# State-space layers: step sizes by way of PSUM, spread of C at the begin of its phase, u in the bank of z, another order of the work

## The reference, cut to what matters

```python
xz = x @ in_w
u, z = jnp.split(xz, 2, axis=-1)
uc = cb + sum((up[:, k:k + L, :] * cw[:, k] for k in range(D_CONV)))
u = jax.nn.silu(uc)
proj = u @ xpw                      # dt (8), Bm (16), Cm (16)
delta = jax.nn.softplus(dt @ dtw + dtb)
def step(h, inp):
    dA = jnp.exp(d_t[..., None] * A)
    h = dA * h + (d_t * u_t)[..., None] * b_t[:, None, :]
    y = jnp.einsum('bdn,bn->bd', h, c_t)
y = (ys + u * Dp) * jax.nn.silu(z)
x = _layer_norm(y @ ow + x, ln_w[i], ln_b[i])
```

## Time and profile before

| | us |
|---|---|
| median of three runs | 626.53 |
| the three runs | 626.53, 624.88, 626.65 |
| the profiled execution | 624.93 |
| its span in the trace | 623.1 |

### The profile page before, as it was taken

How to read it: one execution, slowest core, us unless ns; L and a number is a source line. 1 busy time by engine, 2 the same in 40 slices (tenths; PEclk the granted TensorE clock), 3 DMA queues, 4 the chain that set the end, 5 groups by cost and what they waited for, 6 DMA issues and landing times.

```text
span 623.1 us, 21724 instructions
## 1 busy us (share of the span) xinstructions
PE 525.9 (84%) x8989; PEld 416.4 (67%) x8989; DVE 442.8 (71%) x1737; ACT 322.1 (52%) x952; POOL 147.9 (24%) x197
## 2 busy tenths in 40 slices
PE   6979968779995999999999999997588888888668
PEld 4646644468883888888888888885466666566355
DVE  2888749865445777777777777772489889898851
ACT  2778748236554344444444444343567766678411
POOL 4255625137001000000000000000624656335500
PEclk9979979699995555555555555555599999999775
DMA  8910000010003000000000000000000000000000
GB/s 317 420 50 1 3 5 1 2 49 1 1 0 103 4 5 4 4 4 4 5 4 5 4 5 4 4 5 1 1 1 2 1 3 2 2 1 2 1 1 8
DMA packets 6306, 16.13 MB, mean 26 GB/s; under 512 B 2680, under 2 KB 3488, under 8 KB 5696
## 3 DMA queue, kind: packets, MB, share of 16 engines
q1 hardware_dynamic: 5792, 14.48, 6.3%
q10 hardware_dynamic: 416, 0.26, 0.1%
HBM read 14.61 MB, written 0.13 MB: 24 GB/s over the span
## 4 chain that ended last, share of the span: by engine, by line
PE 42%; DVE 33%; ACT 15%; issue 8%; POOL 1%; DMA 1%; DVEq 0%; ACTq 0%; POOLq 0%
PE bank L1713 7%; PE bank L1807 6%; ACT esp L699 3%; PE bank L1643 3%; PE bank L1656 3%; DVE ssum L1233 2%; ACT a L686 2%; PE bank L1511 2%; DVE w L1288 2%; ACT e L701 2%; DVE qblk L1288 2%; PE bank L1919 2%; PE bank L1905 2%; DVE rz L1268 2%; DVE opre L1209 2%
## 5 line engine op out<-in xcount | busy, mean ns | idle before, releaser
L1713 PE MATMUL bank<-esp,qblk 128*128 128x1 f16 (+1 forms) x2048 | 66.6, 166 | 12.0 <-ACT esp L699 12.0
L1713 PEld LDWEIGHTS bank<-esp,qblk 128*128 128x128 f16 x2048 | 61.2, 104 | 17.3 <-ACT esp L699 17.3
L1713 PE MATMUL bank<-hsp,kT 128*128 128x2 f16 x2048 | 63.5, 166 | 2.0 <-DVE hsp L1261 1.9
L1713 PEld LDWEIGHTS bank<-hsp,kT 128*128 128x128 f16 x2048 | 59.5, 104 | 2.1 <-issue 2.1
L686 ACT ACTIVATE a<-opre 128x4 f32<-128x4 f32 x64 | 13.1, 205 | 80.8 <-DVE opre L1212 80.8
L488 POOL MEMSET ctxT<- 128x128 f32 x1 | 0.3, 313 | 229.7 <-DVE xres L1275 229.7
L693 ACT ACTIVATE gact<-bank,lgate 128x16 f32<-128x16 f32 x64 | 17.5, 274 | 45.6 <-PE bank L1713 45.6
L1288 DVE TENSOR_TENSOR_SCAN qblk<-ctxT,bank 128x512 f32<-128x512 f32 x32 | 36.8, 1202 | 3.9 <-PE bank L1905 3.6
L1288 DVE TENSOR_TENSOR_SCAN w<-kT,bank 128x512 f32<-128x512 f32 x32 | 36.7, 1201 | 1.9 <-PE bank L1905 1.6
L509 POOL TENSOR_TENSOR kT<-T,aneg 128x496 f32<-128x496 f32 x32 | 32.2, 1040 | 20.1 <-DVE T L1367 20.1
L1713 PEld LDWEIGHTS bank<-asp,lsp 128*128 128x128 f16 x768 | 25.4, 105 | 17.1 <-DVE asp L1223 16.8
(11 more groups left out here) (333 smaller groups left out, 1379.4 us busy)
## 6 DMA issues: line engine op xcount, KB each, us to landing
w<-in_w_dram SPq DMA_DIRECT2D x2, 2048.0 KB
ctxT<-in_ctxT_dram SPq DMA_DIRECT2D x8, 256.0 KB, 6.3
wqkv<-in_qkvT_dram SPq DMA_DIRECT2D x1, 1536.0 KB, 12.1
w<-in_mw_dram SPq DMA_DIRECT2D x1, 1024.0 KB, 4.8
lw<-in_lw_dram SPq DMA_DIRECT2D x1, 960.0 KB, 24.2
rows<-in_rows_dram SPq DMA_DIRECT2D x1, 772.0 KB, 8.9
wqkv<-in_fw_dram SPq DMA_DIRECT2D x1, 532.0 KB, 3.7
T<-in_mask_dram SPq DMA_DIRECT2D x1, 512.0 KB, 6.2
```

The source lines that it names most:

```text
L1713: return pe.matmul(out, lhsT, rhs, start=start, stop=stop, skip_group_check=True)
```

## The change

Step sizes: `steps_of_time` writes `m_dps`, the free half of PSUM bank 5; `times_u` reads it there, and a new VectorE instruction, `copied_steps`, copies it to `delta` in SBUF for GpSimd, which waits for that copy. `du` is signalled first, the copy second. The turned x and u move from bank 5 to bank 6, so the bias of the time steps can be put into bank 5 at the begin of a phase. `turn_c` writes to bank 6, behind the turning of du, and both it and `spread_c` now run at the begin of the phase that uses them. `spread_c` stands between `centred` and `normalised`. On TensorE, `turned` newly waits for the spread, `project_z` for `padded_u`, `time_bias` for the copied steps; `conv_bias` stands behind `turned`, `project_z` behind the second `scan_input`, `skip_y` ahead of states 5 to 7, `turn_du` behind `project_out`. On VectorE, `gate` comes ahead of the steps, and `ratio` behind the copy of state 3. On ScalarE, exp 1 stands behind `turned_x`, exp 2 behind `padded_u`, exp 5 behind the sigmoid of u, and the copy of state 6 ahead of `squares`.

```diff
 TURNED_ACT, TURNED_DVE = B * (XG - 1), B
+BY_ACT, BY_DVE = (0, 2, 4, 6), (1, 3, 5, 7)
 m_in = w1[:, 0:ML * 2 * MI]
...
 m_inv = m_a1 = bank[6][:, TOK:2 * TOK]
+m_dps = bank[5][:, TOK:2 * TOK]
...
                            pat(own4, [[0, NG], [1, BT], [0, CK]]), ALU.mult).then_inc(sem["m_dg"], 1)
-        pool.wait_ge(sem["m_delta"], 2 * c + 1)
+        pool.wait_ge(sem["m_delta"], 2 * c + 2)
         for i in range(NT):
...
     def turned_x(c):
         act.wait_ge(sem["m_xt"], c + 1)
-        act.activation(m_xT[c % 2], bank[5][:, 0:P], ACT.Copy).then_inc(sem["m_xp"], 1)
+        act.activation(m_xT[c % 2], bank[6][:, 0:P], ACT.Copy).then_inc(sem["m_xp"], 1)
     def padded_u(c):
         act.wait_ge(sem["m_uz"], 2 * c + 1)
-        act.activation(upad[:, c % 2, :, :, MK - 1:], bank[5][:, P:P + TOK].rearrange("p (c b t) -> p c b t", c=MC, b=BT),
+        act.activation(upad[:, c % 2, :, :, MK - 1:], bank[6][:, TOK:2 * TOK].rearrange("p (c b t) -> p c b t", c=MC, b=BT),
                        ACT.Copy).then_inc(sem["m_up"], 1)
     def sigmoid(to, of):
...
         c = q + 1 if q + 1 < 2 * ML else None
-        decays(q, 0, 2)
+        decays(q, 0, 1)
         if q:
...
             turned_x(c)
-        decays(q, 2, 3)
+        decays(q, 1, 2)
         if c:
             padded_u(c)
-        decays(q, 3, 4)
+        decays(q, 2, 4)
         turned_state(q, 0)
-        decays(q, 4, 6)
+        decays(q, 4, 5)
         if c:
             sigmoid_u(c)
-        decays(q, 6, 7)
+        decays(q, 5, 7)
         if c:
...
         turned_state(q, 4)
+        turned_state(q, 6)
         if c:
             squares(c)
-        turned_state(q, 6)
         turned_y(q)
...
         dve.tensor_tensor(diagcc[c % 2].rearrange("p (n t) -> p n t", t=S),
-                          pat(bank[4][:, 0:1], [[1, MN], [0, S]], TOK + 2 * MN),
+                          pat(bank[6][:, 0:1], [[1, MN], [0, S]]),
                           pat(m32, [[0, MN], [1, S]]), ALU.mult).then_inc(sem["m_prod"], 1)
     def ratio(c):
...
     def steps_of_time(c):
-        dve.scalar_tensor_tensor(out=delta, in0=bank[5][:, 0:TOK], scalar=0.0, in1=m_a2,
-                                 op0=ALU.max, op1=ALU.add).then_inc(sem["m_delta"], 1)
+        step.mark(dve.scalar_tensor_tensor(out=m_dps, in0=bank[5][:, 0:TOK], scalar=0.0, in1=m_a2,
+                                           op0=ALU.max, op1=ALU.add))
     def times_u(c):
-        dve.wait_ge(sem["m_delta"], 2 * c + 1)
-        dve.tensor_tensor(du, delta, m_gate_u[c % 2], ALU.mult).then_inc(sem["m_delta"], 1)
+        step.sync()
+        dve.tensor_tensor(du, m_dps, m_gate_u[c % 2], ALU.mult).then_inc(sem["m_delta"], 1)
+    def copied_steps(c):
+        step.sync()
+        dve.tensor_copy(delta, m_dps).then_inc(sem["m_delta"], 1)
...
     gated_z(0)
-    spread_c(0)
     ratio(0)
...
     times_u(0)
+    copied_steps(0)
     for q in range(2 * ML):
...
             centred(q - 1)
+        spread_c(q)
+        if q:
             normalised(q - 1)
...
         scan(q, 7)
+        turned_state(q, 3)
         if c:
             ratio(c)
-            spread_c(c)
-        turned_state(q, 3)
         turned_state(q, 5)
...
             second_factor(c)
-            steps_of_time(c)
         gate(q)
         if c:
+            steps_of_time(c)
             times_u(c)
+            copied_steps(c)
         residual(q)
...
             pe.wait_ge(sem["ln_xn"], LN_LAST + c)
-        pe.transpose(bank[5][:, 0:P], xn[:, c % 2, :], ident).then_inc(sem["m_xt"], 1)
+        if c:
+            pe.wait_ge(sem["m_prod"], 3 * c)
+            pe.wait_ge(sem["m_duT"], c)
+        pe.transpose(bank[6][:, 0:P], xn[:, c % 2, :], ident).then_inc(sem["m_xt"], 1)
     def project_u(c):
...
             at = (l * 2 * MC + n) * P
-            ins = mm(bank[5][:, (n + 1) * P:(n + 2) * P], m_in[:, at:at + P], m_xT[s], start=(n == 0), stop=True)
+            ins = mm(bank[6][:, (n + 2) * P:(n + 3) * P], m_in[:, at:at + P], m_xT[s], start=(n == 0), stop=True)
         ins.then_inc(sem["m_uz"], 1)
     def project_z(c):
         l, s = divmod(c, 2)
-        if c:
-            pe.wait_ge(sem["m_duT"], c)
+        pe.wait_ge(sem["m_up"], c + 1)
         at = (l * 2 + 1) * MI
...
     def time_bias(c):
-        pe.wait_ge(sem["m_up"], c + 1)
+        if c:
+            pe.wait_ge(sem["m_delta"], 2 * c)
         biases(bank[5], ML * MC + c // 2 * MC)
     def project_bc(c):
...
     def turn_c(c):
         pe.wait_ge(sem["m_dg"], 2 * c + 2)
+        pe.wait_ge(sem["m_duT"], c + 1)
         for n in range(NG):
-            ins = mm(bank[4][n * S:(n + 1) * S, TOK + 2 * MN:TOK + 3 * MN], m32, m_bcm[:, n * MN:(n + 1) * MN],
+            ins = mm(bank[6][n * S:(n + 1) * S, 0:MN], m32, m_bcm[:, n * MN:(n + 1) * MN],
                      start=True, stop=True)
...
     def turn_du(c):
-        pe.wait_ge(sem["m_delta"], 2 * c + 2)
+        pe.wait_ge(sem["m_delta"], 2 * c + 1)
         for ch in range(MC):
...
         ins.then_inc(sem["m_dt"], 1)
+    def copied_state(q, i):
+        if i in BY_ACT:
+            pe.wait_ge(sem["turned_act"], TURNED_ACT + q * len(BY_ACT) + BY_ACT.index(i) + 1)
+        else:
+            pe.wait_ge(sem["turned_dve"], TURNED_DVE + q * len(BY_DVE) + BY_DVE.index(i) + 1)
     def scan_input(q, ch):
...
             if q:
-                pe.wait_ge(sem["turned_act"], TURNED_ACT + q * BT)
-                pe.wait_ge(sem["turned_dve"], TURNED_DVE + q * BT)
+                copied_state(q - 1, BY_ACT[-1])
+                copied_state(q - 1, BY_DVE[-1])
         for b in range(BT):
...
         elif i < BT:
-            own, base = ("turned_act", TURNED_ACT) if i % 2 else ("turned_dve", TURNED_DVE)
-            pe.wait_ge(sem[own], base + q * BT + (i + 1) // 2)
+            copied_state(q, i - 1)
         for k in range(CK):
...
     def skip_y(q):
         l, s = divmod(q, 2)
-        pe.wait_ge(sem["m_prod"], 3 * min(q + 2, 2 * ML))
+        if q + 1 < 2 * ML:
+            pe.wait_ge(sem["m_bcs"], q + 2)
         if q:
...
     def sum_y(q, ch):
-        pe.wait_ge(sem["turned_act"], TURNED_ACT + q * BT + 2 * (ch + 1))
-        pe.wait_ge(sem["turned_dve"], TURNED_DVE + q * BT + 2 * (ch + 1))
+        pe.wait_ge(sem["m_prod"], 3 * q + 3)
+        for by in (BY_ACT, BY_DVE):
+            copied_state(q, max(i for i in by if i // BT == ch))
         for k in range(CK):
...
     conv_bias(0)
+    time_bias(0)
     turned(0)
...
     project_z(0)
-    time_bias(0)
     project_time(0)
     project_bc(0)
-    turn_c(0)
     turn_du(0)
...
         if c:
-            conv_bias(c)
+            time_bias(c)
+        turn_c(q)
         scan_input(q, 0)
...
             turned(c)
+            conv_bias(c)
             project_u(c)
...
         turn_state(q, 1)
+        scan_input(q, 1)
         if c:
             project_z(c)
-        scan_input(q, 1)
-        if c:
-            time_bias(c)
         turn_state(q, 2)
...
             project_bc(c)
-        for i in range(3, 7):
+        for i in range(3, 5):
             turn_state(q, i)
-        if c:
-            turn_c(c)
-        turn_state(q, 7)
         skip_y(q)
+        for i in range(5, 8):
+            turn_state(q, i)
         sum_y(q, 0)
...
         turn_y(q)
+        project_out(q)
         if c:
             turn_du(c)
-        project_out(q)
...
     pe.wait_ge(sem["ln_xT"], transposed(LN_LAST + 1 + 2 * ML))

```

## The result

The changed kernel took 620.47 us (median of 20 runs) against 625.52 for the kernel before (20 runs); the ratio of the two is 0.9924, with a 95% interval of 0.9908 to 0.9939. That is 4.75 us by the ratio and 5.05 by the medians; the forecast was 4.05. The profiled execution took 621.16 (span 619.4). Two of the changed kernel's 20 runs took 626.6 and 626.9 while the others lie between 618.5 and 622.5; one run of the kernel before took 989.56, which a median does not feel.

The account below looks back on a forecast made before the run. VectorE, busy 17.27 of 19.10 us in a steady phase, was taken as nearly full. Six phases −3.0, first phase −1.15, last +0.1 gave −4.05: 622.5 us against a median of 626.53, range 618.5 to 628.

Parts of the forecast that it names:

- Spread of C moved: VectorE, each phase: 0.60 us saved in the last stretch, normalised 0.10 later because the spread now stands before it.
- Steps, du, copy: VectorE behind the gate: du 0.42 instead of 1.07, copy about 0.40, all beside the output projection; residual 0.25 earlier.
- du behind the output projection: TensorE turns du as the projection drains (0.44); the scan input ends at G+4.2, tying with the first scan.
- GpSimd later: GpSimd's multiplies start 1.55 later; scans stall 0.17 and 0.04 behind exps 1 and 2, at no cost.
- Fifth scan, +0.12: VectorE, steady phase: the fifth scan starts at G+10.26 against 10.14, behind the second scan input.
- The slower rival: Other work overflows the TensorE and ScalarE chain from normalised to gating of u: 628.8 us; chance 0.13.
- the first rival: VectorE's count decides, copy and moved spread not hidden: 0.10 saved per phase, 625.2 us, no measurable change; chance 0.17.
- Gate, −0.02: End of a phase: with the gate ahead of the steps, it comes 1.27 after the last copy instead of 1.29.
- Start, −1.15: Up to the first gate: 1.19 saved at ratio, 0.6 by the phase; bias pairs cost 0.4 and 0.2.
- Last phase and tail, +0.1 and 0: Last phase loses 0.1 at the first scan; nothing changes behind the last gate.
- the clock as a rival: TensorE's granted clock falls in steady phases, costing some 2 us per phase: 634 us or more; chance 0.04.

Follow-up runs that it names:

- e2: Changed kernel with the spread of C and its turning put back at the end of the phase, skip product behind state 7: 630.91 us.
- e4: Changed kernel without the way by PSUM: steps written to SBUF at once, no copy, GpSimd released by the steps: 621.04 us.
- e8: Changed kernel with ScalarE's exp 1 moved ahead of turned_x and exp 2 ahead of padded_u: 625.60 us.
- e7: Changed kernel with the convolution's bias moved from between turned and project_u to one phase ahead, between turn_y and project_out: 625.68 us.
- e12: Kernel before, with unread matmuls put into TensorE's waits at the start, in each phase, in the last phase and in the tail: 625.42 us.
- e6: Changed kernel with only the first time bias put back between the first project_z and project_time: 621.24 us.
- e1: The changed kernel run again, unaltered: 620.49 us.
- e5: The kernel before run again, unaltered, for a second profile: 624.73 us, one run.
- e9: Changed kernel with unread matmul pairs in TensorE's waits: 8 behind the first project_bc, 10 in the last phase, 8 behind the last project_out: 620.75 us.
- e3: Changed kernel with only the skip product put back behind state 7: 619.19 us.
- e10: Changed kernel with the edits of e6, e7, e8 and e9 together: 617.40 us.
- e11: The kernel of e10 with two more unread matmul pairs in every phase, around sum_y's second half: 613.61 us.

## Why the prediction was right in its sum and wrong in its split

- *Spread of C moved* (−0.60 in the last stretch, +0.10 at normalised). Right: from the fifth scan to the gate a phase takes 8.34 where it took 8.88, with the 0.06 of the gate in it; normalised is 0.05 later. e2 gives 0.48 for it on VectorE; its other 0.24 is a wait of TensorE that belongs to that edit.
- *Steps, du, copy; du behind the output projection; GpSimd later.* Times right to 0.05. The way by PSUM, the copy and GpSimd's later start are worth nothing: e4, with the residual at the same G+2.14. The premise that the route by PSUM mattered to du was empty.
- *Fifth scan, +0.12.* Measured +0.32. It is the mis-sized term of the steady phase. I had found exp 2's stall at 0.04 and called it free, as the gating of u came later. I had also put TensorE's wait behind turned at 0.7 and covered the bias pair with it: in the kernel before, turned and that wait take 0.69 together, and the wait alone 0.37, while the pair takes 0.70. So the pair overhung ScalarE's copy, project_u started at G+5.17 and not 5.04, exp 2 with it; the third scan came 0.26 late, and the fourth scan's end then set the second scan input. e8 gives 0.27 for the order of the exps and e7 0.10 for the bias pair. The slower rival named this chain; it held for a fraction of its size. By its size alone, 0.22 per phase, the change lies nearer to the 0.10 of the first rival than to the 0.50 forecast, though not by that rival's mechanism (e4).
- *Gate, −0.02.* Measured +0.06 (1.35 after the last copy for 1.29). TensorE's half of sum_y ends 0.13 ahead of the gate, where it was 0.06. It is 0.13 or 0.14 in every profile with the new order, and 0.07 in e12, where the gate waits too; why is open. With the fifth scan's 0.20 it makes up the 0.28 between 18.52 and 18.80.
- *Start, −1.15* (its terms as listed add up to −1.19). The 1.19 at ratio came; the bias pairs cost 0.81 and not 0.4 (e6: 0.83), and the bias pair between turned and project_u at half clock overhung by 0.7 where I had 0.2. Of the 1.15, 0.25 was left.
- *Last phase and tail, +0.1 and 0.* Wrong, and the larger error: −1.26 and −2.38. I priced the clock as a rival in one direction only, as a loss in steady phases. It gave back 3.6 us at the end, where the trace of before already showed 0.50 (a scan input at 2.09). That the points of its rise and fall moved, and that they are worth this much, is shown by e1, e5, e9 and e12; which part of the change moved them is open: not the skip product (e3), not the way by PSUM (e4). It hangs on little: e6, e7 and e8, each one edit away, had the end of the kernel before in their profiles.

Without the last phase and the tail the change is worth 1.6 us, a quarter of a per cent, less than the 0.3% that a measurement of this kernel tells. The forecast of a clear gain held because of a mechanism that it did not contain: that the sum came out is luck.

## What to carry to other kernels

Before costing a change, mark in the profile where TensorE's granted clock is below 1.00, and treat each such stretch as able to go either way; an order that is 0.27 us per phase better (e8) can measure as nothing when it moves a fall of the clock into a phase. Then compare stage by stage between fixed points of the work, and not by the total. Where an in-order engine has instructions of two chains, a stall that seems covered is worth a second look at what starts at its end: here a scan input that may only begin when the fourth scan is over. And a few matmuls that nobody reads, placed in waits that have room for them, can pay, together with an order that uses the clock they keep: two pairs per phase took 3.8 us off (e10 to e11). By themselves they gained nothing, neither in the changed kernel (e9) nor in the one before (e12).

## What the runs showed of the hardware

- The granted clock fell from 1.00 to 0.50 inside a phase in seven profiled phases (e2, e6, e7, e8, e9, and twice e10; the last phases not counted), each time 2.9 to 3.2 us behind the gate, stayed there for 6.8 us and cost 2.2 to 2.8 us. What TensorE did before it fell was thin: two waits around the gate (0.45 and 0.61 in all but e2), then transposes, a bias of 16 rows and one projection. That is not enough by itself, as the phases that did not fall have the same waits. With two pairs of full 128-row matmuls in those waits it did not fall in eight phases (e11). In e10 TensorE was issuing nearly without a gap from G+0.5 on and the clock fell all the same. The Trainium skill, "TensorE: Matmul & The Clock Gate", section "HAM oscillation", has a kernel whose waits throw the clock back again and again, waits several times as long as the longest here (0.80, in e2, in the 8 us ahead of a fall); e10 and e11 agree that filling waits keeps it up, with the addition that only some phases of one kernel, and by e6 and e7 only some of its executions, are hit.
- A VectorE multiplication of two SBUF operands does not run beside GpSimd's multiply in these traces; the one that started later waits. In e12 du started 0.68 after GpSimd and took 0.62, in the kernel before 0.22 after it and took 1.07; both end 1.3 after GpSimd's start, whose single multiply takes 1.02, and GpSimd's next one then takes 1.2. Started 40 ns ahead of GpSimd, du takes 0.43, and it is GpSimd's first multiply that takes 1.26 (e4). Timeline of e12: GpSimd, gate, du.

```profile
466.44 3.16 POOL L509 TENSOR_TENSOR kT<-T,aneg 128x496 f32<-128x496 f32 x3 [5.10 <-DVE T L1367]
...
466.77 0.42 DVE L1302 TENSOR_TENSOR T<-bank,T 128x256 f32<-128x256 f32 x1 [0.41 <-PE bank L1807]
467.12 0.62 DVE L1372 TENSOR_TENSOR T<-T 128x256 f32<-128x256 f32 x1
```

The Trainium skill, "SBUF — State Buffer", section "SBUF: two separate sides", says that a VectorE operation with two SBUF inputs and a GpSimd operation that reads SBUF share a pair of ports, and that the one that starts first holds it for its whole instruction; these rows agree.
